# Cross-attention over 1500 keys: the product of sums split over two slots, its followers moved, and another order in the prologue

## What is computed

```python
x = (hidden - mu) * rsqrt(var + LN_EPS) * ln_gamma + ln_beta
Q = split_heads(x @ Wq.T)                      # 32 heads of 16
scores = einsum('bhsd,bhtd->bhst', Q, K) * HEAD_DIM ** -0.5
probs = softmax(where(mask, scores, -inf))     # over 1500 keys
attn = einsum('bhst,bhtd->bhsd', probs, V)
out = hidden + attn @ Wout.T
```

## Time and profile before

| | us |
|---|---|
| median of three runs | 1595.49 |
| profiled execution, its own time | 1601.01 |
| its span | 1599.3 |
| TensorE busy | 1432.5 |
| GpSimd busy | 1121.6 |
| VectorE busy | 1074.8 |
| ScalarE busy | 753.0 |

### The profile page before, as it was taken

The page is one execution under the profiler, slowest core; times in us unless marked ns, Lnnn a source line. Parts: engine busy times, 40 slices in busy tenths (PEclk is TensorE's granted clock), DMA queues, the critical chain, the costliest instruction groups (busy, mean ns, idle before and its releaser), DMA issues.

```text
span 1599.3 us, 66930 instructions
## 1 busy us (share of the span) xinstructions
PE 1432.5 (90%) x30464; PEld 1057.1 (66%) x30464; DVE 1074.8 (67%) x3356; ACT 753.0 (47%) x623; POOL 1121.6 (70%) x403
## 2 busy tenths in 40 slices
PE   4878989899999999999998999999998999999886
PEld 3335667667676666767676766767676676767675
DVE  6334767677777677777776767777777777777730
ACT  1123545455555445454554544555554544555553
POOL 1002768787877687877777777787777878777786
PEclk7887999999999899999999989999999999999999
DMA  9101444444444444443435444444444444444320
GB/s 292 54 0 64 154 159 152 148 151 149 147 143 150 151 163 140 154 156 142 160 127 174 153 138 146 152 147 141 151 165 165 152 146 161 150 154 145 132 90 7
DMA packets 39164, 224.94 MB, mean 141 GB/s; under 512 B 4546, under 2 KB 4578, under 8 KB 26882
## 3 DMA queue, kind: packets, MB, share of 16 engines
q1 hardware_dynamic: 38882, 220.68, 40.8%
HBM read 216.90 MB, written 3.77 MB: 138 GB/s over the span
## 4 chain that ended last, share of the span: by engine, by line
PE 71%; ACT 15%; DVE 8%; issue 5%; DMA 1%; SPq 0%; POOL 0%; ACTq 0%; POOLq 0%; DVEq 0%
PE ps L276 21%; PE ps L237 15%; ACT probs L359 14%; PE ps L291 14%; PE ps L305 7%; DVE masked L324 6%; PE ps L268 5%; PE ps L253 4%; PE ps L652 4%; DVE den_inv L348 1%; ACT sums L610 1%; DMA probs<-in_x 1%; DVE stats L540 0%; DVE tile_max L324 0%; ACTq L358 0%
## 5 line engine op out<-in xcount | busy, mean ns | idle before, releaser
L324 DVE CUSTOM_DVE_ANT_0 masked<-ps,mask_tile 112x500 bf16<-112x500 f32 x1536 | 978.3, 672 | 438.8 <-PE ps L237 422.9
L359 ACT ACTIVATE probs<-ps,mask_bias 125x1792 f32<-125x1792 f32 x384 | 673.7, 1754 | 712.3 <-PE ps L276 712.2
L405 POOL TENSOR_TENSOR sums<-probs 125x1792 f32<-125x1792 f32 x128 | 512.1, 4001 | 439.2 <-ACT probs L359 439.2
L237 PE MATMUL ps<-kT,qdb 32*112 32x500 bf16 x1536 | 528.1, 415 | 45.6 <-DVE tile_max L324 31.6
L276 PE MATMUL ps<-qd,kT 32*125 32x112 f32 x12288 | 517.6, 278 | 10.3 <-issue 10.3
L409 POOL TENSOR_TENSOR sums<-sums,probs 125x1792 f32<-125x1792 f32 x128 | 510.3, 3986 | 14.6 <-ACT probs L359 5.3
L276 PEld LDWEIGHTS ps<-qd,kT 32*125 32x125 f32 x12288 | 497.1, 186 | 12.3 <-issue 11.2
L291 PE MATMUL ps<-probs,v 125*32 125x112 f32 x12288 | 382.1, 264 | 4.6 <-issue 4.3
L291 PEld LDWEIGHTS ps<-probs,v 125*32 125x32 f32 x12288 | 301.5, 111 | 81.3 <-issue 64.9
L237 PEld LDWEIGHTS ps<-kT,qdb 32*112 32x112 bf16 x1536 | 162.4, 124 | 183.5 <-DVE tile_max L324 129.1
L268 PE MATMUL ps<-max_rows,ones_row 4*125 4x448 bf16 x1536 | 177.2, 397 | 72.5 <-ACT probs L359 71.3
(11 more groups left out here) (45 smaller groups left out, 246.1 us busy)
## 6 DMA issues: line engine op xcount, KB each, us to landing
kT<-in_kt SPq DMA_DIRECT2D x96, 1000.0 KB, 6.4
v<-in_ctx SPq DMA_DIRECT2D x96, 1000.0 KB
mask_tile<-mask_add SPq DMA_DIRECT2D x32, 328.1 KB, 15.3
x_res<-in_x SPq DMA_DIRECT2D x16, 224.0 KB, 15.8
out<-result SPq DMA_DIRECT2D x16, 224.0 KB, 15.5
probs<-in_x SPq DMA_DIRECT2D x14, 224.0 KB, 8.8
v<-in_wq_t SPq DMA_DIRECT2D x1, 1024.0 KB, 5.6
woutT<-in_wout_t SPq DMA_DIRECT2D x1, 1024.0 KB, 20.6
```

The costliest lines, as they stand in the source:

```text
L237: nc.tensor.matmul(bank[0:PAIR_Q, 0:KEYS], qdb[rows, b % 2, g, :], keys, start=True, stop=True).then_inc(ring_filled, 1)
L324: nc.vector.tensor_tensor_reduce(out=masked[0:PAIR_Q, t % 2, :], in0=bank[0:PAIR_Q, 0:KEYS], in1=mask_tile[0:PAIR_Q, b % 2, KEYS * c:KEYS ...
L359: nc.scalar.activation(probs[0:LANES, k % PROBS], ps[0:LANES, 0:TILES_R, 0:BANK_Q], ACT.Exp, bias=mask_bias[0:LANES, n:n + 1], scale=SCALE ...
L405: nc.gpsimd.tensor_tensor(total, probs[0:LANES, slot % PROBS], probs[0:LANES, (slot + 1) % PROBS], ALU.add).then_inc(summed, 1)
```

## The change

Three things are changed.

- The product of a sum with the ones is cut by e. Its first half stays in slots 5, 8, 11 and 2 of the next batch; its second half goes to slots 6, 9, and 0 and 3 of the next batch. The inversions, which need all of it, go from behind tiles (2,3), (3,1), (3,3), (4,1) to (3,3), (4,0), (4,2), (4,3), written as (slot, tile).
- The projection's quarters go from slot 9 of an even batch and slots 0, 1, 3 of the odd batch behind it to slot 10 of the even and 1, 3, 4 of the odd one.
- In the prologue VectorE normalises each unit right behind its statistics, with ScalarE's roots at other places among its copies. The first tiles no longer stand in fours behind the query fills of units 1 to 4, but singly behind each matmul (two behind the fourth) of the query fills of units 2 to 4.

```diff
-INVERT_AT = [(2, 3), (3, 1), (3, 3), (4, 1)]
+INVERT_AT = [(3, 3), (4, 0), (4, 2), (4, 3)]
-OUT_AT = [(0, 9), (1, 0), (1, 1), (1, 3)]
+OUT_AT = [(0, 10), (1, 1), (1, 3), (1, 4)]
+TILES_FROM_UNIT = 2
+STD_AFTER = [("q", 0, 3), ("x", 1, 3), ("q", 1, 0), ("q", 1, 1)]
...
-        def add_denominators(pe, b, j):
-
-            pe.wait_ge(summed, 2 * (SUMS * b + j) + 2)
-            if j == 0:
+        def add_denominators(pe, b, j, e):
+
+            if e == 0:
+                pe.wait_ge(summed, 2 * (SUMS * b + j) + 2)
+            if j == 0 and e == 0:
                 wait_over(pe, den_taken, BLOCKS * b)
-            for e in range(2):
-                for r in range(TILES_R):
...
+            for r in range(TILES_R):
...
+            if e == 1:
+                mm.then_inc(den_done, 1)
...
             for u in range(1, UNITS):
                 statistics(u)
-            for u in range(1, UNITS):
                 normalise(u)
...
-                    if (u, c) == (0, BLOCKS - 1):
-                        for later_unit in range(1, UNITS):
-                            std(later_unit)
+                if (kind, u, c) in STD_AFTER:
+                    std(STD_AFTER.index((kind, u, c)) + 1)
...
-                mm.then_inc(filled, 1)
-                if u > 0:
-                    for unit in FIRST_TILES[tile:tile + 4]:
+                    if h == BLOCKS - 1:
+                        mm.then_inc(filled, 1)
+                    for unit in FIRST_TILES[tile:tile + (h + 5) // 4] if u >= TILES_FROM_UNIT else ():
                         score_tile(pe, unit)
-                    tile += 4
+                        tile += 1
...
-                    if k >= 5 and k % 3 == 2:
-                        add_denominators(pe, b, k // 3 - 1)
-                    elif k == 2 and b > 0:
-                        add_denominators(pe, b - 1, SUMS - 1)
+                    if k >= 5 and k % 3 != 1:
+                        add_denominators(pe, b, (k - 5) // 3, (k - 5) % 3)
+                    elif k in (0, 2, 3) and b > 0:
+                        add_denominators(pe, b - 1, (k + SLOTS - 5) // 3, (k + SLOTS - 5) % 3)
```

More of the change, by code:

```diff
@@ L295, in times_values @@
             mm.then_inc(pv_done, 1)
-        def add_denominators(pe, b, j):
-            pe.wait_ge(summed, 2 * (SUMS * b + j) + 2)
-            if j == 0:
+        def add_denominators(pe, b, j, e):
+            if e == 0:
+                pe.wait_ge(summed, 2 * (SUMS * b + j) + 2)
+            if j == 0 and e == 0:
                 wait_over(pe, den_taken, BLOCKS * b)
-            for e in range(2):
-                for r in range(TILES_R):
[L304 to L308, removed]
+            for r in range(TILES_R):
+                own_q = sums[0:LANES, j % 2, r, :].rearrange("p (g e q) -> p g e q", g=BLOCKS, e=2)[:, :, e, :]
+                mm = nc.tensor.matmul(den[ROW * r:ROW * (r + 1), :, :], ones[0:LANES, e, :], own_q,
+                                      start=(j == 0 and e == 0), stop=(j == SUMS - 1 and e == 1),
+                                      skip_group_check=True, tile_position=(0, ROW * r))
+            if e == 1:
+                mm.then_inc(den_done, 1)
         def take_unit(dve, unit):
@@ L691, in _ @@
             times_values(pe, end, SLOTS - 1)
-            add_denominators(pe, end, SUMS - 1)
+            add_denominators(pe, end, SUMS - 2, 1)
+            for e in range(2):
+                add_denominators(pe, end, SUMS - 1, e)
             for part in range(OUT_PARTS):
```

## The result

The changed kernel takes 1552.07 us (median of 4 runs, 1548.39 to 1557.35) against 1595.42 for the kernel before in the same comparison (4 runs, 1591.05 to 1601.37). The ratio is 0.9728, 95% interval 0.9686 to 0.9771: 43 us faster. The forecast was 1547 in a range from 1525 to 1576.

The account below looks back on a forecast made before the run. Bound by the TensorE and ScalarE loop over the single copy of the four score banks. Prologue -23 and main loop -26 (-0.83 times 31 batches) make -49 from the 1595.5 median: 1547 us, range 1525 to 1576.

Parts of the forecast that it names:

- Start of unit 1: Prologue: x ready near 18.1, so unit 1's transpositions start there instead of at 27.20 us; -9.1 us.
- Unit 1's fills: Prologue: unit 1's four query fills without tiles take 14.5 us instead of 24.4; -9.9 us (-6 to -15).
- Units 2 to 4: Prologue: spread tiles no longer wait on the ring, and one slow fill regains the clock; together -4 us (0 to -9).
- The clock: Prologue, units 2 to 4: one slow query fill of up to three regains the full clock, 1.7 us.
- The tiles and the ring: Prologue, units 2 to 4: 56 spread tiles cost 17.9 us instead of 20.8, the ring of two no longer stalling TensorE; -2.9.
- the rival of the changes between shapes: Prologue: each lone tile between full-array matmuls changes array shape at a cost; 12 us lost, time 1559; chance 0.08.
- The halves: Main loop: slots 2, 5, 8 save 0.32 each, slot 11 0.20; halves in 0, 6, 9 cost nothing; -1.16 per batch.
- The quarters: Main loop: moved projection quarters cost net +0.49 us per even batch (slot 10 to 4.94) and +0.06 per odd batch.
- The inversions: Main loop, slot 4 of even batches: three inversions there may make a tile behind the scores late; +0.1 us.
- The likeliest case: Whole kernel: both prologue and main loop changes act, 1530 to 1565 us; chance 0.77.
- the second rival: Main loop gives nothing: half plus tile doesn't fit 0.53 us, slot 4's inversions delay slot 5; 1572 us; chance 0.11.
- The slower rival: Main loop: a half product costs as much as a whole, mostly fixed cost; 1622 us; chance 0.04.

Follow-up runs that it names:

- the experiment: Changed kernel with VectorE's and ScalarE's old prologue order (all statistics, then all normalisations), tiles at their new places: 1560.41 us, ratio 0.9790 to the kernel before.
- the quarter back: Changed kernel with the first projection quarter back in slot 9 of even batches, beside the half product: 1539.97 us, ratio 0.9686 to the kernel before.
- halves in 7 and 8: Changed kernel with the second sum's halves in slots 7 and 8, first quarter in slot 9 of even batches: 1525.02 us, ratio 0.9567 to the kernel before.
- all improvements together: Changed kernel with prologue tiles in pairs, second sum's halves in slots 7 and 8, first quarter in even slot 9: 1514.62 us, ratio 0.9524 to before.

## Why the prediction was right, and where it was off

**Start of unit 1, -9.1.** Right: 27.20 to 18.57 is 8.6 in the profiles, 9.0 by the experiment.

**Unit 1's fills, -9.9.** From the first query fill to the transpositions of unit 2, 24.4 us became 11.4: -13.0. The mechanism held. The size was off because the clock rose early in these fills (0.50 from 21.86 to 26.40 and 1.00 from there on): 11.4 is near the lower bound of 9.2.

**Units 2 to 4, -4.** 79.9 us (54.86 to 134.71) became 71.7 (33.24 to 104.92): -8.2. Two terms were mis-sized in opposite directions, and added up from the rows the whole gain is the clock's. These are the slow fills of before:

```profile
58.70 4.90 PE L652 MATMUL ps<-sums,v 128*128 128x448 f32 x8 [0.91 <-ACT sums L610]
...
85.23 5.29 PE L652 MATMUL ps<-sums,v 128*128 128x448 f32 x8 [0.91 <-ACT sums L610]
...
119.06 4.97 PE L652 MATMUL ps<-sums,v 128*128 128x448 f32 x8
...
126.11 7.97 PE L652 MATMUL ps<-sums,v 128*128 128x448 f32 x16
```

The clock, forecast at -1.7. With the one at 92.61 four fills took 1.6 to 2.0 us more than the 3.27 of a fast one, and the last two together 1.5 more than two fast ones: some 8.5 us. (None of them ran at the 1.2 GHz level throughout, as I had read the one at 92.61; its mean grant is 0.65.) I had taken one slow fill of up to three as regained. Now the grant is 1.00 from 33.24 to 104.92, in the fills behind the transpositions too, which I had said would stay slow. The rule of the Trainium skill, page "TensorE: Matmul & The Clock Gate", section "A second HAM failure mode: psum-queue depth-cycling", on short idles between groups, agrees with that in kind. The gain is larger than the 5.1 us that I had worked out by it, because more fills were slow than I had looked at.

The tiles and the ring, forecast at -2.9. Before, four tiles stood between two fills for 2.15 us, ten times: 21.5. Now there are 45 places of one or two tiles with 0.35 each, 15.8: a gain of 5.7. But a matmul ahead of such a place takes 0.95, where I had counted 0.80, and 45 such places are some 6.8 us. (The 0.80 was a quarter of a run of four, which holds one change already; one more in a run takes 0.75.) So the rival of the changes between shapes was partly true, if not with the 12 us that I had put on it, and the ring and the changes together gave nothing, about +1. The transpositions with the gap behind them are 0.6 us shorter in all, also with the clock. The rule of the Trainium skill, page "TensorEngine Tiling (Array Packing)", section "Key Properties", that a change of tiling mode drains TensorE, agrees with these traces (0.20 ahead of the tile, and 0.35 until the next matmul whether one tile stands between or two). My argument against it was wrong: I looked only behind the tile, and the 0.20 stands ahead of it.

**The halves, -1.16 per batch.** Slots 2 and 8 fell to 3.43, 11 to 3.52, and slots 0 and 6 took their half for nothing, in both parities. Odd slot 5 fell too. The step that failed is "The halves that arrive in slots 0, 6 and 9 find 0.53 us idle: 0": for slot 9 it costs some 0.3 in slot 10 in all batches (5.29 against 4.98 without the half in even ones). I had looked at TensorE's idle time alone, and not at what VectorE had to do behind the late tile.

**The quarters, +0.49 and +0.06.** Even slots 9 and 10: 3.43 and 5.30, so 8.73 against 7.88, +0.85; in the kernel without the half in slot 9 they are 3.43 and 4.98, +0.53, near the 0.49 forecast. Odd: 3.43, 3.93, 4.31 and 3.93 in slots 0, 1, 3 and 4 against 3.99, 3.93, 4.35 and 3.43: -0.10. The 0.15 for inversions in odd slot 4 did not appear; the slot is long enough for VectorE.

**The inversions, +0.1.** Probably 0.27 in even batches, one slot later than where I put them. Slot 5 of even batches, with its half product, stands at 3.70 and 3.97, above the 3.5 that I had named as a sign of being wrong: for this slot it came true.

**The sum.** Even batches were forecast at -0.57 and came to -0.07, odd at -1.10 and came to -0.98; the mean is -0.53 instead of -0.83, 16 us instead of 26. The prologue gave 29.8 in the profiles, 23 forecast, and some 26 by the runs of the kernel with that part alone. So the loop gave 10 us less than forecast or more, the prologue 3 to 7 more, and the total, 43 against 49, is closer than its parts: in part that is luck. The likeliest case was right; the second rival, a loop that gives nothing, is refuted by the loop alone (upper end of its ratio 0.9979) and by its slots, but in even batches it came close (-0.07). The slower rival fell with the first row: a half product takes 0.40 (1125.62, until the next row at 1126.02).

## What to carry to other kernels

Where the distance between two events of a loop is as regular as here, price each kind of slot by it and add up: in three of the experiments (no half in slot 9, the quarter back, halves in 7 and 8) the slots came within 0.1 us of what that gave. Idle time on the engine that gets a moved piece is not enough; follow what stands behind the piece on the next engine, here a reduction over the whole batch that had no slack. And where small work of another shape must go between large matmuls, put two together rather than spread them singly.

## What the runs showed of the hardware

I had not expected that the fp32 matmul of 448 columns ahead of a lone tile would take 0.95 us, against 0.75 for one more in a run, while two tiles behind it cost no more than one (0.35 to the next matmul in both kernels). Nor that the clock would stay at 1.00 from 33.24 to 104.92, over three gaps of 1.6 us behind transpositions; in the trace of all improvements together it fell once behind a shorter one, of 0.78 us.
